# Attention with a mixture of experts: the three groups ahead of the first expert tile overlap one another

## The chip, the cores and the metric

The kernel runs on one core of a Trainium2 chip. The metric is the device time of one execution in microseconds, as the median of several runs. A profile gives the busy intervals of the engines: TensorE (PE, with its weight loads apart as PEld), VectorE (DVE), ScalarE (ACT), GpSimd (POOL) and SyncE (SP, which here only issues DMAs).

## The reference, cut to what matters

```python
x = x + xattn(layernorm(x), ctx, ctx, ...)   # 32 sequences x 128 tokens x 256, 4 heads of 64
x = x + ffn(layernorm(x), router_w, w1, w2)  # 8 experts, 2 for each token, hidden size 1024

# xattn: gates from q and ctx; cs = cumsum(log_sigmoid(fg))
log_D = where(ltr, cs - cs.T, -inf) + ig.T
D = exp(log_D - max(log_D))
C = (q @ k.T / 8) * D
normalizer = maximum(abs(sum(C)), exp(-max_log_D))
h = C / (normalizer + EPS) @ v               # then normed per head, times a scale
# ffn: softmax router, top 2 of 8, h = gelu(x @ w1[e]), y = h @ w2[e], weighed sum
```

## The kernel before, in words

The 32 sequences are worked on in eight groups of four. A group's attention is a long chain over all engines. In the order of a group's own data the pieces are, with their function names (the same name on several engines means the parts of one piece):

- `x_stats`, `x_moments` (DVE), `x_rstd` (POOL), `x_shift` (DVE), `x_norm` (ACT): the layer norm of x, in place in `xin`.
- `turn` (PE, transposes), `turned` (ACT): q transposed. `gates` (PE, 32 small matmuls), `gates_biased` (DVE), `centre` (POOL, the values less their mean), `log_sigmoid` (ACT), `log_forget` (DVE).
- `cumsum`, `decay_turn` (PE), `decay_in`, `cummax`, `rows_right`, `max_token` (DVE; the last three are `middle` there), `rows_left` (ACT), `max_turn` (PE): the terms of the decay.
- `logd` (PE), `decay` (ACT, exp), `scores` (PE, then DVE): C for the four sequences.
- `values` (PE, then ACT: a copy and a square), `head_var` (DVE, six steps), `head_rstd` (POOL), `head_norm`, `head_gamma`, `residual` (DVE): x1.
- `x1_stats`, `x1_moments`, `x1_rstd`, `x1_shift`, `x1_norm`: its layer norm. `router_turn` (PE), `router_turned` (ACT), `logits` (PE), `router` (DVE, 14 steps), `router_exp` (POOL), `meta` (DVE), `ranks`, `counts` (PE), `slots_of`, `list_step` (DVE): which rows go to which expert. `scatter` (POOL, two indirect DMAs for each sequence): the normed rows go to memory, sorted by expert.

Each engine runs its instructions in the order in which they are written; semaphores hold an instruction until its inputs are there, and all that stands behind it on that engine waits too. The order is written out by hand, in `window(w)` for groups 0, 1 and 2 (`STEADY` is 3) and in `step(t, ...)` from t = 3 on. In a step eight expert tiles of 128 rows are computed (`hidden`, `output`, `gelu`, `low`, `weigh`, `add`; 71 tiles in all), and pieces of groups t to t+2 are put between them. In the windows there are no tiles. There the weights of the eight experts are split: each of 16 halves is scaled to 16 bits by ACT (`weights_high`) and its remainder is taken by DVE (`weights_low`); `weights_high(n)` waits for `weights_low(n-1)`. The first `hidden` waits for all 16.

Before, `window(w)` takes group w from its decays to its router, one piece after another: PE has logd(w), scores(w), values(w), turn(w+2), cumsum, decay_turn and max_turn of w+1, gates(w+2), router_turn(w), logits(w). On POOL the eight scatters of group w-1 stand ahead of x_rstd(w+2) and head_rstd(w). On SP, `load_x(g)` waits for turn(g-1), and everything behind it in the queue waits with it.

Of the kernel before, what the change touches and what calls it, by code (L numbers as in the profile page):

```python
# [13 lines left out]
P = 128  # L14
# [67 lines left out]
def build(nc, x, ctx_n, ctx_t, gate_w_in, gate_b_in, gamma, rw_t, w1, w2, cf, cb, pad_rows, out):  # L82
    with ExitStack() as stack:
# [39 lines left out]
        rT = ct[1][:, :, :].rearrange("p a n -> p (a n)").rearrange("p (b j n) -> p b j n", b=G, j=CK)  # L123
# [74 lines left out]
        yo = [sb(f"yo{i}", [P, D]) for i in range(YO)]  # L198
        yx = sb("yx", [P, D])
# [12 lines left out]


# [148 lines left out]
        def _(sp):  # L362
# [68 lines left out]
            for half in range(9, 13):  # L431
                load_w(half)
            sp.dma_start(rows[SPARE:SPARE + P, :], pad_rows).then_inc(s_spare, 16)
            sp.dma_start(out[NT:NT + P, :], pad_rows[:, 0:D]).then_inc(s_spare, 16)
            store_x1(0)
            for half in range(13, 2 * NE):
                load_w(half)
            load_x(3)
            load_x_again(1)
            load_c(2)  # L440
            load_k(3)
            store_x1(1)
            load_c(3)
            load_x(4)
# [33 lines left out]
        def _(pe):  # L478
# [69 lines left out]
            def logd(g, few):  # L548
                if few[0] == 0:
# [4 lines left out]
                    if g < STEADY:  # L554
# [62 lines left out]
            def logits(g):  # L617
# [5 lines left out]
                for b in range(G):  # L623
                    pe.wait_ge(s_rTc, 2 * g + b // 2 + 1)
                    for j in range(CK):
                        mm = pe.matmul(LG[:, b * NE:(b + 1) * NE], rT[:, b, j, :], rwT[:, j, :],  # L626
# [81 lines left out]
            def middle(g):  # L708
                cumsum(g)
                decay_turn(g)  # L710
                max_turn(g)

            def window(w):
                logd(w, (0, 1, 2))
                if w > 0:
                    ranks(w - 1)
                if w > 1:
                    counts(w - 1)
                scores(w, 0)
                logd(w, (3,))  # L720
                scores(w, 1)
                if w == 0:
                    turn(1, 0)
                    turn(1, 1)
                for b in range(G):
                    values(w, b)
                if w == 0:
                    gates(1)
                turn(w + 2, 0)
                turn(w + 2, 1)  # L730
                middle(w + 1)
# [8 lines left out]
            middle(0)  # L740
            pe.wait_ge(s_cbf, 16)
            window(0)
# [4 lines left out]
            def step(t, w, m, f, r):  # L747
                if w is not None:
                    logd(w, (0, 1, 2))
                if r is not None:  # L750
                    ranks(r)
                    if r > 0:
                        counts(r)
                for j in slots(t):
# [5 lines left out]
                    if j == 0 and w is not None:  # L760
# [4 lines left out]
                    if j == 0 and w is not None:  # L765
# [37 lines left out]
        def _(act):  # L803
# [43 lines left out]
            def decay(g, b):  # L847
# [4 lines left out]
                if b == 2:  # L852
# [36 lines left out]
            def router_turned(g, h):  # L889
                act.wait_ge(s_rt, 2 * g + h + 1)  # L890
                if h == 0:
                    act.wait_ge(s_pv, 4 * g + 4)
                act.activation(rT[:, 2 * h:2 * h + 2, :, :],
# [17 lines left out]
            def weigh(i):  # L911
# [3 lines left out]
                act.activation(yx[:, :], YX, ACT.Copy, scale=cw[i % RW][:, :]).then_inc(s_yx, 1)  # L915

            def window(w):
                first = 2 + 5 * w
                floor(w)
                for b in range(G - 1):  # L920
                    decay(w, b)
                weights_high(first)
                if w == 0:
                    x_norm(1, 0)
                    x_norm(1, 1)
                decay(w, G - 1)
                if w == 0:
                    turned(1, 0)
                    turned(1, 1)
                weights_high(first + 1)  # L930
                values(w, 0)
                weights_high(first + 2)
                for b in range(1, G):
                    values(w, b)
                x_norm(w + 2, 0)
                x_norm(w + 2, 1)
                log_sigmoid(w + 1)
                turned(w + 2, 0)
                turned(w + 2, 1)
                rows_left(w + 1)  # L940
                x1_norm(w, 0)
                x1_norm(w, 1)
                weights_high(first + 3)
                router_turned(w, 0)
                router_turned(w, 1)
                if w < 2:
# [723 lines left out]
```

## Time and profile before

| | |
|---|---|
| median of 3 runs | 699.69 us (697.93 to 702.44) |
| the profiled execution | 696.18 us |
| its span, first to last instruction | 694.3 us |
| busy: PE, PEld, DVE, ACT, POOL | 607.4, 480.4, 371.6, 343.2, 265.4 us |
| mean granted TensorE clock | 0.90 |

The span is what the profile's rows are measured in; the execution lasts 1.9 us longer, and the median of the runs 3.5 us longer than this one execution. Times within the rows are counted from the start of the span. A row of a timeline gives the start, the length from the first start to the last end, the engine, the line, the operation, the tiles written and read, how many instructions are merged in it and, in brackets, how long the engine sat idle before it and what released it. The clock column is the granted TensorE clock, 1.00 for 2.4 GHz and 0.50 for 1.2 GHz.

### The profile page before, as it was taken

The numbers are of one execution on the slowest core, as the hardware profiler recorded it, in microseconds if no ns is written. First come the engines' busy times: TensorE is split into PE (matmuls) and PEld (weight loads), VectorE is DVE, ScalarE is ACT, GpSimd is POOL, SyncE is SP. The second block draws the span as 40 slices with busy tenths as digits, with TensorE's granted clock in tenths as the row PEclk, the third lists the DMA queues.
The fourth block names the chain that finished last, engine by engine and source line by source line (L and its number), as shares of the span: only waits on it lengthen the run. The fifth ranks groups of instructions, "written<-read, shape, count | busy, mean of one in ns | idle before, by whom it ended". The sixth has DMA issues, their size and how long they took to land.

```text
span 694.3 us, 18994 instructions
## 1 busy us (share of the span) xinstructions
PE 607.4 (87%) x5885; PEld 480.4 (69%) x5885; DVE 371.6 (54%) x1132; ACT 343.2 (49%) x684; POOL 265.4 (38%) x198
## 2 busy tenths in 40 slices
PE   3775857928899999999899999999899999999993
PEld 3365556626777776777687778678678788787872
DVE  1554664864395539544944584476464444444441
ACT  3453554433457455745564546556345455555551
POOL 0113271542355256434733363444362222222222
PEclk9985555555899999999999999999999999999998
DMA  9995523203324343424333233314244333233222
GB/s 301 380 353 184 199 84 122 70 23 114 109 65 93 60 116 90 102 33 124 106 58 72 46 94 55 85 41 101 42 92 107 59 49 54 47 50 49 48 25 24
DMA packets 44233, 68.14 MB, mean 98 GB/s; under 512 B 4832, under 2 KB 35808, under 8 KB 44000
## 3 DMA queue, kind: packets, MB, share of 16 engines
q1 hardware_dynamic: 30848, 49.09, 22.6%
q0 software_dynamic: 13296, 17.83, 15.1%
q8 instruction: 60, 0.98, 0.6%
q14 instruction: 29, 0.24, 0.1%
HBM read 44.89 MB, written 23.35 MB: 98 GB/s over the span
## 4 chain that ended last, share of the span: by engine, by line
PE 65%; issue 12%; POOL 9%; DVE 6%; ACT 5%; DMA 2%; SPq 0%; DVEq 0%; POOLq 0%; ACTq 0%
PE bank L704 15%; PE bank L690 9%; PE bank L692 8%; PE bank L691 7%; PE bank L705 7%; PE bank L626 3%; POOL rows L1532 3%; PE bank L567 3%; PE bank L652 3%; PE bank L513 2%; PE bank L595 2%; PE bank L580 2%; POOL out L1542 2%; POOL hrs L1519 1%; PE bank L563 1%
## 5 line engine op out<-in xcount | busy, mean ns | idle before, releaser
L690 PE MATMUL bank<-xT,wall 128*128 128x128 f16 x1136 | 209.1, 220 | 9.8 <-issue 9.5
L692 PE MATMUL bank<-xT,wall 128*128 128x128 f16 x1136 | 209.1, 220 | 0.0
L691 PE MATMUL bank<-xT,wall 128*128 128x128 f16 x1136 | 209.1, 220 | 0.0
L704 PE MATMUL bank<-wall,ffn 128*128 x568 | 192.9, 380 | 3.9 <-DVE yo L1309 3.7
L1542 POOL DMA_INDIRECT out<-yo,dst x71 | 114.8, 1618 | 199.7 <-DVE yo L1309 128.4
L900 ACT ACTIVATE ffn<-bank 128x512 f32<-128x512 f32 x142 | 84.7, 596 | 182.3 <-PE bank L692 181.1
L1303 DVE TENSOR_TENSOR gl<-ffn 128x512 f16<-128x512 f32 x94 | 64.9, 690 | 133.5 <-ACT ffn L902 69.9
L690 PEld LDWEIGHTS bank<-xT,wall 128*128 x1136 | 112.5, 99 | 30.3 <-issue 16.7
L692 PEld LDWEIGHTS bank<-xT,wall 128*128 x1136 | 111.3, 98 | 1.9
L691 PEld LDWEIGHTS bank<-xT,wall 128*128 x1136 | 111.3, 98 | 1.1
L705 PE MATMUL bank<-wall,gl 128*128 x376 | 102.4, 272 | 0.0
L704 PEld LDWEIGHTS bank<-wall,ffn 128*128 128x128 f16 x568 | 56.0, 99 | 61.3 <-issue 9.6
L1532 POOL DMA_INDIRECT rows<-rowb,slot x64 | 76.3, 1192 | 55.1 <-DVE rowb L1214 38.9
L902 ACT ACTIVATE ffn<-bank 128x512 f16<-128x512 f32 x142 | 84.0, 591 | 0.0
L1303 DVE TENSOR_TENSOR ffn<-ffn 128x512 f16<-128x512 f32 x48 | 33.1, 690 | 65.6 <-ACT ffn L902 34.7
L705 PE MATMUL bank<-wall,ffn 128*128 x192 | 52.6, 274 | 0.0
L915 ACT ACTIVATE yx<-bank,cw 128x256 f32<-128x256 f32 x71 | 33.7, 474 | 24.5 <-PE bank L705 24.5
L499 PE MATMUL bank<-cst,xin 128*128 128x128 f32 x64 | 12.9, 369 | 37.4 <-ACT xin L811 37.4
L595 PE MATMUL bank<-vt,ct 128*128 128x65 f32 x256 | 39.2, 317 | 2.7 <-DVE ct L1073 2.7
L595 PEld LDWEIGHTS bank<-vt,ct 128*128 128x128 f32 x256 | 37.6, 233 | 4.3 <-DVE ct L1073 3.4
L705 PEld LDWEIGHTS bank<-wall,gl 128*128 128x128 f16 x376 | 36.7, 98 | 3.3
L1309 DVE SCALAR_TENSOR_TENSOR yo<-bank,cw,yx 128x256 f32<-128x256 f32 x71 | 34.2, 482 | 8.5 <-ACT yx L915 4.7
(139 smaller groups left out, 883.9 us busy)
## 6 DMA issues: line engine op xcount, KB each, us to landing
wall<-in_w SPq DMA_DIRECT2D x15, 1024.0 KB, 11.5
xrow<-rows SPq DMA_DIRECT2D x71, 130.0 KB, 2.4
xin<-in_x SPq DMA_DIRECT2D x8, 512.0 KB, 4.4
kT<-in_ctx_t SPq DMA_DIRECT2D x8, 512.0 KB, 4.4
ctn<-in_ctx SPq DMA_DIRECT2D x8, 512.0 KB, 4.2
xres<-in_x SPq DMA_DIRECT2D x8, 512.0 KB, 4.7
out<-xres SPq DMA_DIRECT2D x8, 512.0 KB, 3.6
rows<-in_const_pad SPq DMA_DIRECT2D x9, 130.0 KB, 2.5
```

The costliest lines, as they stand in the source:

```text
L595: mm = pe.matmul(VB[b][:, h4 * (DH + 1):(h4 + 1) * (DH + 1)], ct[b // 2][:, h4 % 2, c0:c0 + P], vt[:, b, h4, :], start=True, stop=True)
L690: pe.matmul(o, hi, xT[i % XT][:, c, :], start=(c == 0), stop=False)
L691: pe.matmul(o, hi, xT[i % XT][:, CK + c, :], start=False, stop=False)
L692: mm = pe.matmul(o, lo, xT[i % XT][:, c, :], start=False, stop=(c == CK - 1))
L704: pe.matmul(YB[:, :], gh[q][:, m4, :], weights(i, w, 2 * D), start=(a == 0 and m4 == 0), stop=False)
L705: mm = pe.matmul(Y, gl[q][:, m4, :], weights(i, w, D), start=False, stop=(a == 1 and m4 == 3))
L900: act.activation(gf[a], HB[a][:, :], ACT.Gelu, scale=1.0 / WSCALE).then_inc(s_gf, 1)
L902: act.activation(gh[(2 * i + a) % HR][:, :, :], HB[a][:, :].rearrange("p (m n) -> p m n", m=4), ACT.Gelu, scale=1.0 / WSCALE).then_inc(s_g ...
L1303: dve.tensor_tensor(gl[q][:, :, :], gf[a].rearrange("p (m n) -> p m n", m=4), gh[q][:, :, :], ALU.subtract).then_inc(s_glo, 1)
L1309: dve.scalar_tensor_tensor(yo[i % YO][:, :], Y, cw[i % RW][:, :], yx[:, :], ALU.mult, ALU.add).then_inc(s_yo, 1)
L1532: pool.indirect_dma_start(out=rows[:, :], out_offset=bass.IndirectOffsetOnAxis(ap=slot[:, k, b:b + 1], axis=0), in_=rowb[:, b, :], in_offs ...
L1542: pool.indirect_dma_start(out=out[:, :], out_offset=bass.IndirectOffsetOnAxis(ap=dst[i % RW][:, 0:1], axis=0), in_=yo[i % YO][:, :], in_of ...
```

## The change

The windows are shifted by half a group. Ahead of window 0 the decays and scores of group 0 are made (a new helper `attend` on PE) and x of group 1 is normed and turned. `window(w)` then holds: values(w) and all that follows to logits(w); in between, the last terms of the decay of group w+1, its logd, decays and scores; gates(w+2); and x_norm(w+3). So at the first tile the scores of group 3 are there, and step 3 holds neither its decays nor its scores; `ranks(2)` and `counts(2)` move behind the first `hidden`. `gates(w+2)` now stands behind `attend(w+1)` and ahead of `router_turn(w)`.

On DVE scores(w+1, 0) stands between head_gamma(w) and residual(w), scores(w+1, 1) ahead of x1_shift(w), and the 15 list steps of window 2 now stand behind head_var. On POOL only four of the eight scatters stand ahead of head_rstd(w), the other four behind it. `weights_low`: three halves are split ahead of window 0, four in each window; in window 2 half 14 comes ahead of `router` and half 15 behind it, and their `weights_high` behind `router_turned(2)`. On SP load_x(3) and load_x(4), the weights 12 to 15 and the contexts are reordered. The transposed rows of the router (`rT`) use the buffers of the expert output in groups 0 to 2, so they no longer share a buffer with the decays.

```diff
 PE
-                logd(w, (0, 1, 2))
+                values(w, 0)
+                values(w, 1)
                 if w > 0:
                     ranks(w - 1)
...
+                    turn(w + 2, 0)
+                    turn(w + 2, 1)
+                    cumsum(w + 1)
+                values(w, 2)
+                if w > 0:
+                    decay_turn(w + 1)
+                values(w, 3)
...
+                max_turn(w + 1)
+                attend(w + 1)
                 gates(w + 2)
                 router_turn(w, 0)
                 router_turn(w, 1)
 DVE, window(w)
+                    decay_in(w + 1)
+                    weights_low(first - 1)
+                    middle(w + 1)
...
+                for n in range(6):
+                    head_var(w, n)
...
                 head_norm(w)
                 head_gamma(w)
+                scores(w + 1, 0, 0)
+                scores(w + 1, 0, 1)
                 residual(w)
                 x1_stats(w)
                 x1_moments(w)
+                scores(w + 1, 1, 0)
+                scores(w + 1, 1, 1)
+                x1_shift(w)
...
+                weights_low(first + 2)
                 for n in range(14):
                     router(w, n)
                 meta(w, 0)
+                if w == STEADY - 1:
+                    weights_low(first + 3)
 POOL, window(w)
-                    for b in range(G):
-                        scatter(w - 1, b)
-                x_rstd(w + 2)
+                    scatter(w - 1, 0)
+                    scatter(w - 1, 1)
                 head_rstd(w)
+                    scatter(w - 1, 2)
+                    scatter(w - 1, 3)
                 x1_rstd(w)
```

## Rows read from the trace of the kernel before

**Rows 1.** Page, the span in 40 slices: granted TensorE clock.
```profile
PEclk9985555555899999999999999999999999999998
```
**Rows 2.** Windows by stage: length, busy us (instructions) by engine, clock, DMA, GB/s.
```profile
26.00:75.60 49.60, 35.04 (x184) 28.76 (x185) 26.12 (x53) 24.61 (x41) 10.53 (x8) 0.72 0.86 301
75.60:121.20 45.60, 32.76 (x151) 26.31 (x152) 27.85 (x66) 21.46 (x35) 20.17 (x15) 0.50 0.30 102
121.20:170.20 49.00, 32.72 (x151) 26.29 (x152) 31.11 (x84) 19.82 (x34) 20.34 (x15) 0.50 0.24 73
...
175.00:187.90 12.90, 11.23 (x118) 9.45 (x119) 4.72 (x15) 6.64 (x16) 3.97 (x4) 0.98 0.46 143
187.90:694.30 506.40, 481.18 (x5225) 378.67 (x5224) 270.10 (x870) 260.71 (x546) 205.81 (x145) 0.99 0.33 68
```
**Rows 3.** Chain that ended last, window 1: start, us, what.
```profile
75.81 0.20 DVE lg L1139
...
83.17 1.21 POOL rows L1532
...
94.37 2.77 POOL rows L1532
...
98.54 2.88 POOL hrs L1519
```
**Rows 4.** Timeline of PE, logits(0) to values(1), at 1.2 GHz.
```profile
72.21 3.56 PE L626 MATMUL bank<-rwT,ct 128*128 128x8 f32 x16 [1.26 <-ACT ct L893]
75.62 1.44 PE L563 MATMUL bank<-cbf 128*128 128x512 bf16 x3
...
80.24 2.08 PE L580 MATMUL bank<-qT,kT 64*128 64x128 f32 x16 [0.94 <-ACT ct L854]
...
84.79 2.08 PE L580 MATMUL bank<-qT,kT 64*128 64x128 f32 x16
86.80 7.09 PE L595 MATMUL bank<-vt,ct 128*128 128x65 f32 x32
```
**Rows 5.** Timeline of PE, gates(3) in window 1: first and last of eight rows.
```profile
105.78 0.99 PE L513 MATMUL bank<-gate_w,qT 128*128 128x12 f32 x4
...
111.74 1.01 PE L513 MATMUL bank<-gate_w,kT 128*128 128x12 f32 x4
```
**Rows 6.** Timeline of PE, gates(1) in window 0: first and last of eight rows.
```profile
43.24 0.57 PE L513 MATMUL bank<-gate_w,qT 128*128 128x12 f32 x4
...
46.34 0.59 PE L513 MATMUL bank<-gate_w,kT 128*128 128x12 f32 x4
```
**Rows 7.** Timeline of DVE, window 0: a weight half, first and last of head_var.
```profile
48.79 2.29 DVE L1080 SCALAR_TENSOR_TENSOR wall<-wall 128x2048 f16<-128x2048 f32 x1 [2.04 <-ACT wall L874]
51.00 0.18 DVE L1220 SCALAR_TENSOR_TENSOR n<-u 128x16 f32<-128x16 f32 x1
...
52.91 0.17 DVE L1240 SCALAR_TENSOR_TENSOR hv<-ss,n 128x16 f32<-128x16 f32 x1
```
**Rows 8.** Timeline of DVE, windows 1 and 2: head_norm, first and last list step.
```profile
103.36 1.22 DVE L1054 TENSOR_TENSOR u<-u,hrs 128x1024 f32<-128x1024 f32 x1
...
141.79 0.42 DVE L1258 TENSOR_TENSOR qT<-ncnt,cst 128x256 f32<-128x256 f32 x1
...
145.54 0.17 DVE L1295 TENSOR_TENSOR dn<-up,te 128x8 f32<-128x8 f32 x1
```
**Rows 9.** Timeline of POOL, window 0: x_rstd(2).
```profile
44.66 2.17 POOL L1495 TENSOR_SCALAR ve<-mv 128x4 f32<-128x4 f32 x1 [12.52 <-DVE mv L1027]
46.92 1.04 POOL L1499 TENSOR_TENSOR rs<-ve,mhalf 128x4 f32<-128x4 f32 x1
```
**Rows 10.** Timeline of ACT: weights_high of one half.
```profile
69.70 1.89 ACT L876 ACTIVATE wall<-wall 128x2048 f16<-128x2048 f32 x1
```
**Rows 11.** Timeline of PE, step 3: first scores and last values of group 3.
```profile
177.23 1.16 PE L580 MATMUL bank<-qT,kT 64*128 64x128 f32 x16
...
184.93 3.14 PE L595 MATMUL bank<-vt,ct 128*128 128x65 f32 x24 [1.55 <-DVE ct L1073]
```

More of the change, by code:

```diff
@@ L430, in _ @@
             load_k(2)
-            for half in range(9, 13):
+            for half in range(9, 12):
+                load_w(half)
+            load_x(3)
+            for half in range(12, 14):
                 load_w(half)
@@ L739, in _ @@
             gates(0)
-            middle(0)
+            cumsum(0)
+            decay_turn(0)
+            max_turn(0)
             pe.wait_ge(s_cbf, 16)
+            attend(0)
+            turn(1, 0)
+            turn(1, 1)
             window(0)
@@ L759, in step @@
                         tile_turn(i + 1)
-                    if j == 0 and w is not None:
+                    if j == 0 and ahead:
+                        ranks(r)
+                        counts(r)
+                    if j == 0 and w is not None and not ahead:
                         scores(w, 0)
@@ L914, in weigh @@
                 after(act, s_yo, i)
-                act.activation(yx[:, :], YX, ACT.Copy, scale=cw[i % RW][:, :]).then_inc(s_yx, 1)
+                act.activation(yx, YX, ACT.Copy, scale=cw[i % RW][:, :]).then_inc(s_yx, 1)
             def window(w):
[L918 to L921, printed above, removed]
+                first = 4 + 4 * w
+                if w == 0:
+                    weights_high(3)
+                values(w, 0)
@@ L926, in window @@
[L926 to L940, printed above, removed]
+                    turned(2, 0)
@@ L941, in window @@
+                    turned(2, 1)
+                    rows_left(1)
+                floor(w + 1)
+                for b in range(G - 1):
+                    decay(w + 1, b)
+                if w < STEADY - 1:
+                    weights_high(first + 1)
+                decay(w + 1, G - 1)
+                if w == STEADY - 1:
+                    turned(w + 2, 0)
+                    turned(w + 2, 1)
                 x1_norm(w, 0)
                 x1_norm(w, 1)
-                weights_high(first + 3)
+                if w == STEADY - 1:
+                    weights_high(first + 1)
@@ L956, in _ @@
             weights_high(1)
+            floor(0)
+            for b in range(G - 1):
+                decay(0, b)
+            weights_high(2)
+            x_norm(1, 0)
+            x_norm(1, 1)
+            decay(0, G - 1)
+            turned(1, 0)
+            turned(1, 1)
             window(0)
@@ L970, in step @@
                     log_sigmoid(m)
-                if w is not None:
+                if w is not None and not ahead:
                     decay(w, G - 1)
@@ L1401, in _ @@
             weights_low(1)
+            x_stats(1)
+            x_moments(1)
+            scores(0, 0, 0)
+            scores(0, 0, 1)
+            x_shift(1)
+            weights_low(2)
+            scores(0, 1, 0)
+            scores(0, 1, 1)
             window(0)
```

166 lines of the change are left out of this document (90 added, 76 removed).

## Prediction

> **What bounds the kernel now.** I read three views. The page's slices and the windows by stage [rows 1, 2] come first: from 187.9 us on PE is busy 481.2 of 506.4 us at a clock of 0.99, so the tiles are bound by PE and little is to be had there. Ahead of that lie three windows of 49.6, 45.6 and 49.0 us in which no engine is full: in window 1 PE has 32.8 of 45.6 us, DVE 27.9, ACT 21.5, POOL 20.2, and half of the PE time is due to the lower clock. That is the picture of a chain, not of a full engine. The chain that ended last [rows 3] says which: logits(0), the router's steps, the eight scatters of the group before (83.17 to 97.14 us), then head_rstd(1), which waited behind them on POOL. The timelines [rows 4 to 9] give the prices.
>
> So the windows are a stretch of about 144 us plus the start of step 3, and the change works only there. I lay the new order out stage by stage, in this execution's time, with PE at 1.2 GHz as it was there.
>
> **Up to 47 us nothing moves.** Ahead of window 0 the new order of every engine is the old one: attend(0), turn(1), x_norm(1) and the halves 0 to 2 stand where they stood.
>
> **Window 0.** x_rstd(2) ends at 47.96 [rows 9]. Before, DVE then still did half 4 (2.29 us) and began head_var at 51.00 [rows 7]. Now half 4 is behind, so head_var (2.1 us, 51.00 to 53.08) runs from 48.1 to 50.2: 2.9 us earlier. Then half 4 (2.3 us) stands ahead of middle(1), and centre(1) runs on POOL next to it. I put max_token(1) at 59.2, where it was at 62.3 (which is 9.3 us behind x_shift; now 11, for half 4). attend(1) starts at 59.4. From logd to the first scores of PE are 4.6 us and to the end of its second scores 11.25 us (75.62 to 86.87) [rows 4]; the first DVE scores start at +6.7, so at 66.1. Here is the price of the new place: head_gamma has ended at 61.5, and DVE stands still until 66.1, with residual(0), x1_stats and the whole router behind it. Scores, residual, stats, moments and the second scores take DVE to 72.0; x1_norm is ready at 74.2. But PE then has gates(2), 70.7 to 77.6: eight rows, 105.78 to 112.75, are 6.9 us [rows 5]. They stood under x1_stats and x1_rstd before and cost nothing; now 3.4 us of them (77.6 less 74.2) lie on the path. router_turn, router_turned and logits (3.56 us [rows 4]) end at 83.2, where logits(0) ended at 75.6. With attend(1) already made, values(1) can start at 83.3 instead of 86.8: gain so far 3.5 us.
>
> **Window 1**, from E = 83.3. ranks(0) must wait for the router's 14 steps on DVE (about 0.22 us each [rows 3]; 4.4 us with the half in front). turn(3), cumsum, values 2 and 3 and max_turn follow, and attend(2) starts at E+11.9 = 95.2. head_var ends at 97.1. Four scatters are now gone from ahead of head_rstd (half of 14 us), which would have it start at once, but weights_low(8) starts on DVE at the same moment. On this core the two exclude each other: the `ve` step of x_rstd(2), one addition on 128x4 elements, took 2.17 us beside a weight half, longer than the power of the same size right behind it, 1.04 us [rows 9]. So head_rstd (2.88 us [rows 3]) ends at 99.4 + 2.8 = 102.2. head_norm (1.22 [rows 8]), head_gamma, scores(2), residual, stats and second scores: 110.1 us. Meanwhile scatters 5 to 8 (5.1 us, about 7 with the same exclusion) hold x1_rstd until 111.3. x1_norm ends at 113.6; gates(3) ends at 115.0 on PE; logits(1) ends at 120.7. Before it ended at 121.2, but with attend(2) still to do (11.2 us). Gain 11.8 us.
>
> The Trainium skill (GPSIMD Engine Reference, section Key points) says that GpSimd shares its SBUF interfaces with VectorE and contends with instructions of two SBUF inputs; the trace agrees, with the 2.17 us above. Without the exclusion this window would be 2.2 us shorter.
>
> **Window 2**, from E = 120.8. The same pattern, with the list steps between head_var and head_norm (141.79 to 145.71, 3.9 us [rows 8]). They lie beside head_rstd, so 1 to 2 us of them remain. logits(2) ends at E+36.2 = 157.0. Then comes a tail that did not exist: weights_high(14) and (15) stand behind router_turned(2), each needs the low half before it, and half 15 stands behind the router's steps on DVE. high(14) 1.9 us [rows 10], low(14) 2.3, router 3.3, low(15) 2.3: the last half ends at E+43.1, 6.9 us behind logits. With 0.7 us for the first tile's table reads as before, the first hidden starts at 164.5. It started at 175.0: 4.8 us behind logits. Gain 10.5 us.
>
> **Step 3.** From the first hidden to that of tile 1 there were 12.9 us [rows 2]: hidden twice, logd(3) and scores (two of 1.16 us [rows 11]), waits for decay and scores, and values in two parts, the last 24 matmuls of 3.14 us behind a wait of 1.55 us. The two scores go (2.3 us), the wait (1.55), and logd and the wait for its exp (2.5, my estimate): 6.5 us stay. To these come ranks and counts (0.5) and about 3 us for the clock: PE will have idled 7 us before this point, so the first hiddens probably run at 1.2 GHz. About 10 us. Gain 2.8 us. Behind that nothing is removed: the same 70 tiles at PE's pace.
>
> **SP and the buffers.** load_x(3) now stands ahead of weights 12 to 15 and waits for turn(2), near 52 us; weights 14 and 15 wait for x1_norm(0), near 74, and are needed near 148. k(4) is there at 112 and needed at 144. load_rows(0) waits for centre(3), near 149, and its tile is turned after 157. No load is on the path. The waits for the shared router buffer are met long before. I cost these at nothing; if one cover fails it is a load of some 4 us, once.
>
> **Sum.** 10.5 + 2.8 = 13.3 us of 696.2, so 682.9 us for such an execution. The median of the runs stands 3.5 us above it, so 686 us, 1.9% faster. About 1% (7 us) is what a measurement of this kernel can tell from no change.
>
> **Rivals.**
> 1. *The windows run at 2.4 GHz.* Gates at the upper level take 3.7 us (43.24 to 46.93 [rows 6]) against 6.9. At that level the gates no longer hold router_turn, logits and turns halve: some 7 us for each of windows 1 and 2 and up to 6 in window 0. Full effect: 666 us; in one window only: 679 us. For it: PE's pauses of 7 and more us before turn(w+2) are gone. Against it: from 72.2 to 93.9 us PE was busy with pauses of about 1 us [rows 4] and the clock stayed at 0.50 [rows 2]. Chance 0.2 for all of its forms.
> The Trainium skill (TensorE: Matmul & The Clock Gate, section Why this matters for your kernels) has it that TensorE reaches its upper clock by steady work and loses it by idle gaps; by that rule this rival would be the rule and not the exception, and the stretch just named speaks against it.
> 2. *The gain is eaten in place.* The waits I priced come out longer: DVE behind scores(w+1, 0), POOL's four scatters in front of x1_rstd, the weight tail. Each is 3 to 7 us per window in my layout, so 3 us more in each of windows 1 and 2 leaves 7 us: 692 us and above. Chance 0.2.
> 3. *Slower: the two chains are serial after all.* If in-order waiting makes windows 1 and 2 as long as before (45.6 and 49.0 us), logits(2) ends at 83.2 + 94.6 = 177.8, the first hidden starts at 185.4 and tile 1 near 195.4 instead of 187.9: 7.5 us slower, 707 us. It decides from the point where the two windows together save under 7.5 of 94.6 us; I have 21. Against it: half of the scatters leave the head's path. Chance 0.07.
> 4. *The change does not reach the end,* since step 3 waits for something else (group 5's x, the scatters of group 2): 696 to 700 us. PE is busy 481 of 506 us from there, so a late piece would have to stop it for 10 us. Chance 0.05; it counts as within 1%.
>
> **How the numbers follow.** My layout has 0.48, and its own range is 681 to 692. The clock rival has 0.2, rival 2 0.2 (half of it above 693), the others 0.12. Leaving out half of each outer case gives 671 to 694. Faster by over 1% (under 692.7): 0.48 + 0.2 + a part of rival 2 = 0.78. Within 1%: 0.15. Slower: 0.07.
>
> **What would show it.** The first hidden near 164 us, tile 1 near 174.5, and 506 us from there to the end. logits(0) near 83, logits(1) near 121, logits(2) near 157. DVE idle for 4 to 5 us between head_gamma(0) and scores(1); gates directly in front of router_turn, with no idle between; weights_low(15) as the last thing before the first hidden, 6 to 7 us behind logits(2). Wrong would be: a granted clock of 1.00 inside windows 1 or 2, a window of 45 us or more, a tile section that grew, or a first hidden released by a load.

## The result, and the profile after

The changed kernel takes 679.5 us (median of 4 runs, 678.85 to 679.74), the kernel before 699.66 us (4 runs beside it, 697.93 to 702.44). The ratio is 0.972, with a 95% interval of 0.968 to 0.976: 2.8% faster, where 1.9% was forecast. The profiled execution took 678.85 us, with a span of 677.1 us and a mean granted clock of 0.905; before it was 696.18, 694.3 and 0.900.

The page of the changed kernel, the granted clock in 40 slices (answers to [rows 1]):

```profile
PEclk9985555555999999999999999999899999999998
```

The windows by stage, cut where the last matmul of logits(0), (1) and (2), the first hidden and tile 1's hidden stand (columns as in [rows 2]):

```profile
26.30:81.80 55.50, 45.06 (x229) 33.77 (x229) 32.69 (x66) 27.88 (x49) 13.82 (x10) 0.68 0.85 296
81.80:117.90 36.10, 32.20 (x151) 26.30 (x151) 27.46 (x66) 19.18 (x33) 21.27 (x15) 0.50 0.32 104
117.90:155.10 37.20, 32.38 (x151) 26.36 (x152) 30.09 (x76) 18.76 (x30) 16.46 (x13) 0.50 0.30 96
155.10:162.10 7.00, 0.51 (x2) 0.10 (x1) 6.12 (x22) 4.00 (x6) 1.01 (x1) 0.50 0.00 0
162.10:170.80 8.70, 8.66 (x91) 8.61 (x92) 2.65 (x15) 3.48 (x9) 2.86 (x3) 0.76 0.44 125
170.80:677.10 506.30, 479.61 (x5225) 377.42 (x5222) 270.77 (x870) 260.69 (x546) 206.76 (x147) 0.99 0.33 69
```

Against [rows 2]: logits(0) ends 6.2 us later than before (attend(1) and gates(2) now stand ahead of it), windows 1 and 2 are 36.1 and 37.2 us long instead of 45.6 and 49.0, and the tile section is 506.3 us, as it was. PE's busy time in the windows has not changed (32.2 and 32.4 us against 32.8 and 32.7), only its idle time has: 12.8 and 16.3 us before, 3.9 and 4.8 us now. Behind logits(2) the tail to the first hidden is 7.0 us where it was 4.8, and tile 1's hidden stands 8.5 us behind the first hidden where it was 12.9. Added up: 9.5 and 11.8 us gained in windows 1 and 2, 4.4 in step 3, 6.2 and 2.2 lost in window 0 and in the tail, together 17.3 us of the 17.2 by which the span is shorter.

The predicted places beside the measured ones, in us:

| place | predicted | measured |
|---|---|---|
| max_token(1) | 59.2 | 58.0 |
| scores(1) on DVE; its idle before | 66.1; 4 to 5 | 65.1; 4.56 |
| logits(0) ends | 83.2 | 81.8 |
| head_rstd(1) ends | 102.2 | 99.7 |
| logits(1) ends | 120.7 | 117.9 |
| logits(2) ends | 157.0 | 155.1 |
| first hidden | 164.5 | 162.1 |
| tile 1's hidden | 174.5 | 170.7 |
| from there to the end | 506 | 506.3 |

Timeline of PE in window 0: the last of the eight rows of gates(2), which answer to [rows 5], then the router and the values that follow.

```profile
75.56 1.01 PE L521 MATMUL bank<-gate_w,kT 128*128 128x12 f32 x4
76.41 1.95 PE L621 MATMUL bank<-cst,rowb 128*128 128x128 f32 x8
78.29 3.55 PE L634 MATMUL bank<-rwT,ybuf 128*128 128x8 f32 x16
81.69 3.66 PE L603 MATMUL bank<-vt,ct 128*128 128x65 f32 x16
```

router_turn (L621) follows the gates with no idle; its input, x1_norm, had been ready since 73.16. So 3.25 us of the gates lie on the path, 3.4 were forecast. Timeline of POOL and then DVE in window 1, what answers to [rows 3] and [rows 9]:

```profile
94.81 4.91 POOL L1578 TENSOR_TENSOR hrs<-hv,mhalf 128x16 f32<-128x16 f32 x1 [0.54 <-DVE hv L1284]
99.92 1.98 POOL L1591 DMA_INDIRECT rows<-rowb,slot  x1 [0.19 <-issue]
...
108.06 1.89 POOL L1571 TENSOR_TENSOR vt<-ctn,gsb 128x1024 f32<-128x1024 f32 x1
94.55 0.18 DVE L1284 SCALAR_TENSOR_TENSOR hv<-ss,n 128x16 f32<-128x16 f32 x1
94.64 2.28 DVE L1124 SCALAR_TENSOR_TENSOR wall<-wall 128x2048 f16<-128x2048 f32 x1
...
108.11 1.87 DVE L1093 SCALAR_TENSOR_TENSOR nm<-mv,rs 128x4 f32<-128x4 f32 x1 [0.64 <-POOL rs L1565]
```

head_rstd (L1578) takes 4.91 us beside the weight half (2.28 us, L1124) where it took 2.88 [rows 3]: 2.0 us more, for the exclusion that the prediction priced at 2.2 us. The last row is one that it did not price: x1_shift (L1093), 128x4 elements, takes 1.87 us beside centre (1.89 us, L1571), which starts 0.05 us ahead of it; in window 0, with nothing on POOL beside it, it takes 0.15. The rule of the Trainium skill that the prediction cited (GPSIMD Engine Reference, section Key points: GpSimd shares its SBUF interfaces with VectorE and contends with its instructions of two SBUF inputs) fits both rows.

Timeline of PE and of DVE at the end of window 2:

```profile
151.53 3.55 PE L634 MATMUL bank<-rwT,ybuf 128*128 128x8 f32 x16 [2.22 <-DVE gsb L1137]
162.13 0.28 PE L698 MATMUL bank<-xT,wall 128*128 128x128 f16 x1 [6.53 <-DVE xT L1358]
148.87 2.29 DVE L1128 SCALAR_TENSOR_TENSOR wall<-wall 128x2048 f16<-128x2048 f32 x1 [2.04 <-ACT wall L896]
151.08 0.20 DVE L1137 TENSOR_TENSOR gsb<-bank,gate_b 128x48 f32<-128x48 f32 x1
...
158.65 2.28 DVE L1128 SCALAR_TENSOR_TENSOR wall<-ffn,wall 128x2048 f16<-128x2048 f32 x1
160.85 0.41 DVE L1358 TENSOR_TENSOR xT<-bank,xT 128x256 f16<-128x256 f32 x1
```

logits(2) waits 2.22 us for gates_biased(4) (L1137), which stands behind weight half 13 on DVE (L1128, 148.87). That half had itself waited 2.04 us for its high part on ACT (L896), and the high part had waited for half 12 on DVE, so it is a chain that goes to and fro between the two engines and starts behind x1_shift(2). The first hidden (L698) waits 6.53 us, behind the router, half 15 (158.65) and tile_low (L1358).

### The profile page after: what moved, and what is told of

Read it like the earlier page. It is cut to its first block, busy times and chain, and to the rows that moved or that the text cites. A ratio compares the mean times of both kernels' runs of the same rounds, so it can differ in the third digit from the quotient of the medians.

```text
span 677.1 us, 18991 instructions
## 1 busy us (share of the span) xinstructions
PE 608.8 (90%) x5885; PEld 482.0 (71%) x5885; DVE 377.4 (56%) x1132; ACT 342.5 (51%) x684; POOL 265.7 (39%) x198
## 4 chain that ended last, share of the span: by engine, by line
PE 65%; issue 14%; POOL 8%; DVE 6%; ACT 4%; DMA 1%; SPq 0%; DVEq 0%; POOLq 0%; ACTq 0%
PE bank L712 15%; PE bank L698 9%; PE bank L700 8%; PE bank L699 8%; PE bank L713 8%; PE bank L521 5%; PE bank L603 3%; PE bank L660 3%; POOL rows L1591 2%; POOL out L1601 2%; PE bank L575 2%; POOL hrs L1578 2%; PE bank L588 2%; PE bank L634 1%; PE bank L507 1%
## 5 line engine op out<-in xcount | busy, mean ns | idle before, releaser
L698 PE MATMUL bank<-xT,wall 128*128 128x128 f16 x1136 | 209.4, 220 | 16.3 <-issue 9.7
L1601 POOL DMA_INDIRECT out<-ybuf,dst x71 | 114.7, 1615 | 201.5 <-DVE ybuf L1353 129.7
L698 PEld LDWEIGHTS bank<-xT,wall 128*128 x1136 | 112.6, 99 | 36.5 <-issue 23.1
L1591 POOL DMA_INDIRECT rows<-rowb,slot x64 | 72.7, 1136 | 55.4 <-DVE rowb L1258 39.4
L937 ACT ACTIVATE ybuf<-bank,cw 128x256 f32<-128x256 f32 x71 | 33.6, 474 | 24.5 <-PE bank L713 24.5
L603 PEld LDWEIGHTS bank<-vt,ct 128*128 128x128 f32 x256 | 37.4, 229 | 2.5 <-DVE ct L1117 1.7
L713 PEld LDWEIGHTS bank<-wall,gl 128*128 128x128 f16 x376 | 36.7, 98 | 3.4
L1353 DVE SCALAR_TENSOR_TENSOR ybuf<-bank,cw,ybuf 128x256 f32<-128x256 f32 x71 | 34.3, 483 | 8.5 <-ACT ybuf L937 8.2
L1578 POOL TENSOR_TENSOR hrs<-hv,mhalf 128x16 f32<-128x16 f32 x8 | 25.5, 3190 | 32.7 <-DVE hv L1284 32.7
```

Of the source, the lines that this page charges most:

```text
L603: mm = pe.matmul(VB[b][:, h4 * (DH + 1):(h4 + 1) * (DH + 1)], ct[b // 2][:, h4 % 2, c0:c0 + P], vt[:, b, h4, :], start=True, stop=True)
L698: pe.matmul(o, hi, xT[i % XT][:, c, :], start=(c == 0), stop=False)
L713: mm = pe.matmul(Y, gl[q][:, m4, :], weights(i, w, D), start=False, stop=(a == 1 and m4 == 3))
L1578: pool.tensor_tensor(hrs[:, :], hv[:, :], mhalf[:, :], ALU.pow).then_inc(s_hrs, 1)
L1591: pool.indirect_dma_start(out=rows[:, :], out_offset=bass.IndirectOffsetOnAxis(ap=slot[:, k, b:b + 1], axis=0), in_=rowb[:, b, :], in_offs ...
L1601: pool.indirect_dma_start(out=out[:, :], out_offset=bass.IndirectOffsetOnAxis(ap=dst[i % RW][:, 0:1], axis=0), in_=yo[i % YO], in_offset=N ...
```

## The experiments

The changed kernel is the base of each, but for the second, which starts from the kernel before. The medians of the kernel before beside them were 697.3 to 697.9 us. The changed kernel itself was not run again beside them, so a difference to it of 2 or 3 us is believed only where the places in the trace show it too. Ratios are to the kernel before, with 95% intervals; the last three columns are starts in the profiled execution. Up to logits(0) the executions differ by 1 to 2 us of themselves, in stretches that an edit doesn't touch, so what an edit of windows 1 and 2 does is read from logits(0) on.

| kernel | median us | ratio | span | logits(0) | first hidden | tile 1 |
|---|---|---|---|---|---|---|
| kernel before | 699.7 | | 694.3 | 72.2 | 175.0 | 187.9 |
| changed kernel | 679.5 | 0.972 (0.968 to 0.976) | 677.1 | 78.3 | 162.1 | 170.7 |
| scatters first | 687.7 | 0.987 (0.986 to 0.989) | 684.8 | 79.4 | 170.6 | 178.8 |
| before, scatters split | 697.3 | 0.999 (0.997 to 1.001) | 696.1 | 73.2 | 175.6 | 189.6 |
| half of the gates | 676.4 | 0.971 (0.969 to 0.972) | 674.7 | 75.7 | 158.1 | 167.4 |
| centre late | 677.2 | 0.973 (0.971 to 0.976) | 675.3 | 77.6 | 160.1 | 169.0 |
| half early | 676.1 | 0.969 (0.966 to 0.971) | 673.3 | 78.1 | 159.1 | 167.1 |
| both, and tile_low early | 671.7 | 0.962 (0.960 to 0.964) | 670.1 | 78.4 | 155.4 | 163.9 |
| group 3 late | 684.3 | 0.978 (0.974 to 0.983) | 688.8 | 80.4 | 163.1 | 179.8 |
| the same, again | 686.2 | 0.984 (0.980 to 0.987) | 682.5 | 80.6 | 163.3 | 177.6 |
| fill | 673.0 | 0.964 (0.962 to 0.967) | 670.4 | 71.6 | 156.3 | 164.4 |
| all and fill | 665.9 | 0.955 (0.952 to 0.959) | 664.2 | 71.6 | 149.1 | 157.8 |
| fill in the gates too | 671.1 | 0.962 (0.959 to 0.966) | 668.8 | 73.4 | 153.9 | 162.3 |
| residual first | 679.1 | 0.974 (0.970 to 0.977) | 678.1 | 79.7 | 163.5 | 171.7 |

**All scatters ahead of head_rstd again.**

```diff
                     x_rstd(2)
                 else:
-                    scatter(w - 1, 0)
-                    scatter(w - 1, 1)
+                    for b in range(G):
+                        scatter(w - 1, b)
                 head_rstd(w)
                 if w == 0:
                     centre(1)
-                else:
-                    scatter(w - 1, 2)
-                    scatter(w - 1, 3)
```

> The changed kernel with one part undone: in windows 1 and 2 all eight scatters stand ahead of head_rstd on POOL again. Theory A, the split of the scatters is a large part of the gain: in the changed kernel the first scatter starts at 88.3 us, eight take 14 us (that is what they took before), so head_rstd(1) would start near 102.5 instead of 94.8 and end 5.7 us later; of that x1_rstd, which no longer waits behind four scatters, gives nothing back as long as gates end behind it. Window 1 about 5 us longer, window 2 5 to 6 us longer: 689 to 691 us. Rival B, POOL's order is off the path, as its idle time of 60 per cent would have it: 679 to 681 us.

Measured: 687.7 us, 8.2 more than the changed kernel (7.7 by the spans). Timeline of POOL and DVE, the last scatter, head_rstd(1), head_norm(1):

```profile
100.47 0.96 POOL L1591 DMA_INDIRECT rows<-rowb,slot  x1 [0.30 <-issue]
101.45 2.93 POOL L1578 TENSOR_TENSOR hrs<-hv,mhalf 128x16 f32<-128x16 f32 x1
104.42 1.23 DVE L1098 TENSOR_TENSOR u<-u,hrs 128x1024 f32<-128x1024 f32 x1 [6.36 <-POOL hrs L1578]
```

head_rstd starts at 101.45 instead of 94.81 (1.1 us of this stands ahead of window 1 already), with no wait of its own: it stands behind the scatters, and DVE idles 6.36 us for it where it idled 2.83. From logits(0) to logits(2) are 80.6 us instead of 73.2: 3.6 us more in window 1, 3.8 in window 2. In the new order the split is worth 7 to 8 of the 20 us.

**The split alone, in the kernel before.**

```diff
                     x_rstd(1)
                 else:
-                    for b in range(G):
-                        scatter(w - 1, b)
+                    scatter(w - 1, 0)
+                    scatter(w - 1, 1)
                 x_rstd(w + 2)
                 head_rstd(w)
+                if w > 0:
+                    scatter(w - 1, 2)
+                    scatter(w - 1, 3)
```

> The kernel before with one part of the change alone: in windows 1 and 2 four of the eight scatters stand behind head_rstd. Theory A, as the prediction read the chain of the kernel before (eight scatters, then head_rstd): head_rstd starts up to 5 us earlier in each window and the kernel gains 5 to 9 us: 691 to 695 us. Rival B, before the change head_rstd was bound by its own input as well: head_var ended at 98.3 us, 0.2 us ahead of head_rstd's start in window 1, and at 147.7 against 147.8 in window 2, so the scatters had only just ceased to bind. Then the split gains nothing, and four scatters behind head_rstd delay x1_rstd by up to 1 us in each window: 699 to 702 us.

Measured: 697.25 us over 10 runs against 697.34 for the kernel before. The same split that is worth 7 to 8 us above is worth nothing here. Timeline of POOL in this kernel, head_rstd(1) and (2):

```profile
99.30 2.90 POOL L1519 TENSOR_TENSOR hrs<-hv,mhalf 128x16 f32<-128x16 f32 x1 [5.18 <-DVE hv L1240]
148.34 2.90 POOL L1519 TENSOR_TENSOR hrs<-hv,mhalf 128x16 f32<-128x16 f32 x1 [9.02 <-DVE hv L1240]
```

and of DVE and POOL in the kernel before, which the prediction did not set side by side:

```profile
98.12 0.18 DVE L1240 SCALAR_TENSOR_TENSOR hv<-ss,n 128x16 f32<-128x16 f32 x1
98.52 2.90 POOL L1519 TENSOR_TENSOR hrs<-hv,mhalf 128x16 f32<-128x16 f32 x1
...
147.52 0.17 DVE L1240 SCALAR_TENSOR_TENSOR hv<-ss,n 128x16 f32<-128x16 f32 x1
147.78 2.90 POOL L1519 TENSOR_TENSOR hrs<-hv,mhalf 128x16 f32<-128x16 f32 x1 [3.68 <-DVE hv L1240]
```

Before, head_var(1) ended at 98.30 and head_rstd(1) started at 98.52, so the queue in front of it (the scatters, then x_rstd(3)) was late by 0.2 us at most; in window 2 POOL even waited 3.68 us for head_var. Freed of four scatters, POOL waits 5.18 and 9.02 us. In the changed kernel head_var(1) ends at 94.73; in the run with all scatters first it ends at 95.86, and the scatters hold POOL until 101.43. The overlap brings head_var forward against the router's end, and only then is a queue of scatters in the way.

**Half of the matmuls of gates(2) to gates(4) left out.**

```diff
-                    for j in range(2 * CK):
+                    for j in range(2 * CK) if not 2 <= g < STEADY + 2 else (0, 2 * CK - 1):
```

> The changed kernel with half of the matmuls of gates(2), (3) and (4) left out (two of four for each sequence, so the gates of groups 2 to 4 lack half of their inputs): each gates piece takes about 3.5 us instead of 6.9. Theory A, gates in front of router_turn cost what the prediction says: in window 0 x1_norm ends at 73.2 and gates at 76.4, so router_turn and the end of window 0 move up by 3.2 us; in windows 1 and 2 x1_norm and the weight halves bind nearly as late, so there 0 to 1 us each. Sum 3.2 to 5 us: 674.5 to 676.5 us. Rival B, another wait (the weight half in front of the router on DVE) binds right behind in window 0 too: under 1.5 us, 678 us and above.

The gates of groups 2 to 4 lack half of their inputs in this kernel. Measured: 676.4 us, 3.2 less (2.4 by the spans). Timeline of PE, windows 0 and 2:

```profile
73.54 1.95 PE L621 MATMUL bank<-cst,rowb 128*128 128x128 f32 x8
75.65 3.55 PE L634 MATMUL bank<-rwT,ybuf 128*128 128x8 f32 x16 [0.16 <-DVE gsb L1137]
...
141.80 2.10 PE L621 MATMUL bank<-cst,rowb 128*128 128x128 f32 x8 [1.69 <-ACT rowb L905]
147.51 3.56 PE L634 MATMUL bank<-rwT,ybuf 128*128 128x8 f32 x16 [3.62 <-DVE gsb L1137]
```

In window 0 router_turn comes 2.9 us earlier, about the 3.25 us that the gates held it. In windows 1 and 2 what the gates give up turns into waits: for x1_norm (L621, 1.97 and 1.69 us) and for gates_biased (L634, 0.94 and 3.62 us, where it was none and 2.22). From the second scores on PE to logits are 10.6 and 13.0 us, in the changed kernel 10.7 and 13.0. So PE's gates bind window 0 alone; in window 2 it is the weight halves on DVE and ACT.

**centre behind x1_shift,** so that the small instruction doesn't run beside the large one.

```diff
                 if w > 0:
+                    pool.wait_ge(s_nm2, w + 1)
                     centre(w + 1)
```

> The changed kernel with one wait added: centre(w+1) on POOL waits for x1_shift(w) in windows 1 and 2. In the changed kernel's trace x1_shift, a step of 128x4 elements, takes 1.87 us in windows 1 and 2 beside centre and 0.15 us in window 0. Theory A, the two engines exclude each other: x1_shift takes 0.15 us, x1_norm starts 1.7 us earlier in both windows; in window 1 gates end at 112.4 and x1_norm at 112.1, so nothing is gained there; in window 2 the chain of the last weight halves starts behind x1_shift, so the first tile starts 1.7 us earlier: 677.8 us. Rival B, x1_shift is slow for another reason (its inputs come late): it stays at 1.9 us and the time at 679.5 us.

Measured: 677.2 us, 2.3 less, of which the trace shows 1.6 as the edit's: from logits(1) to logits(2) are 35.6 us instead of 37.2, and window 1 is as long as before (36.0). The other 0.7 stands ahead of logits(0), where nothing was changed. Timeline of DVE and of POOL, window 1:

```profile
107.43 0.16 DVE L1093 SCALAR_TENSOR_TENSOR nm<-mv,rs 128x4 f32<-128x4 f32 x1 [0.64 <-POOL rs L1565]
107.67 3.88 POOL L1571 TENSOR_TENSOR vt<-ctn,gsb 128x1024 f32<-128x1024 f32 x1 [0.28 <-DVE nm L1093]
```

x1_shift is back at 0.16 us; centre now takes 3.88 us beside the next weight half, which nobody waits for. A wait was added, and window 2 became shorter by what x1_shift had lost there.

**A weight half moved from the tail into DVE's idle stretch of window 0,** so that none stands behind router(2).

```diff
                 head_gamma(w)
+                if w == 0:
+                    weights_low(first + 1)
+                    first += 1
                 scores(w + 1, 0, 0)
...
                 meta(w, 0)
-                if w == STEADY - 1:
-                    weights_low(first + 3)
```

ScalarE's high halves move with it, and each later half comes one place earlier.

> The changed kernel with one weight half more split in window 0: half 5 on DVE between head_gamma(0) and scores(1), where DVE sat idle for 4.56 us, and every later half one place earlier, so that none is left behind the router of window 2. Theory A, the first tile waits for the tail of weight halves: weights_low(15) (2.3 us) goes from behind router(2); the first tile then waits for tile_low behind the router, 2.2 us earlier; window 0 itself does not change, since the half fits into the idle time. 677.3 us. Rival B, the half in window 0 pushes scores(1) and the chain of window 0 back by as much, or DVE and ACT are the bound in window 2 whatever the order: 679 to 681 us.

Measured: 676.1 us, 3.4 less (3.8 by the spans). Timeline of DVE in window 0 and of PE at the first hidden:

```profile
60.28 2.28 DVE L1131 SCALAR_TENSOR_TENSOR wall<-wall 128x2048 f16<-128x2048 f32 x1
64.92 1.29 DVE L1120 SCALAR_TENSOR_TENSOR ct<-bank,ct 128x512 f32<-128x512 f32 x2 [2.35 <-PE bank L588]
...
159.12 0.29 PE L698 MATMUL bank<-xT,wall 128*128 128x128 f16 x1 [3.81 <-DVE xT L1361]
```

The idle of 4.56 us takes the half (2.28 us), and the scores behind it start no later; the wait of the first hidden falls from 6.53 to 3.81 us, which is 2.7 of the 3.8 us.

**Both edits, and tile_low(0) ahead of router(2).**

```diff
+                if w == STEADY - 1:
+                    tile_low(0)
                 for n in range(14):
                     router(w, n)
...
             window(2)
-            tile_low(0)
```

> The changed kernel with three edits that each take away one wait found in its trace: the half in window 0 (as in e4_half_early), centre behind x1_shift (as in e3_centre_late), and tile_low(0) ahead of router(2) on DVE, so that the first tile no longer waits for the 14 router steps and meta. If the waits are in series, as the trace shows them (router and last half 5.4 us between logits and the first tile, x1_shift 1.7 us), the first tile starts 5 to 6.5 us earlier than at 162.1 us: 673 to 674.5 us. If they cover each other: 676 us and above.

Measured: 671.7 us, 7.8 less (7.0 by the spans), with 1.27 us left of the wait before the first hidden. Window 2 is 1.6 us shorter, as with centre late, and the stretch from logits(2) to the first hidden is 5.3 us shorter, of which the early half gave 2.7 in its own run; by difference the early tile_low gives 2.5, though it has no run of its own. The gains add up.

**Group 3's logd, decays and scores back in step 3,** where they were before.

```diff
                 max_turn(w + 1)
-                attend(w + 1)
+                if w < STEADY - 1:
+                    attend(w + 1)
```

The same condition stands on ScalarE and VectorE, and the three of them do the work in step 3 instead.

> The changed kernel with group 3 taken out of the overlap: its logd, decays and scores are in step 3 again, as before the change. Theory A: step 3 gets its 12.9 us from the first hidden to that of tile 1 back, where the changed kernel has 8.7 us: 4.2 us lost; window 2 loses scores(3) on DVE (2.5 us), so x1_norm and the chain of weight halves behind it come 1.5 to 2.5 us earlier. Net 2 us slower than the changed kernel: 681.5 us. Rival B: attend(3) is free in window 2 (PE has it in time that it would idle), so the whole 4.2 us are lost: 683.7 us. Rival C: PE has the work to do at some time anyway, and at the higher clock in step 3 it is cheaper: 679 us or less.

> The same kernel as e6_group3_late once more, since its four times lay between 681.3 and 690.6 us. There the second half of values(3) and the first hidden of tile 1 ran at half pace behind a wait of 1.55 us in step 3 (5.39 us for 24 matmuls). If that wait lets the clock fall in some executions only, the times spread again over 5 to 9 us, the lowest near 681.3 us; a median of 682 to 685 us. If the first look was disturbed: all within 2 us of 681.5 us.

Measured: 684.3 us, but spread from 681.3 to 690.6, and in the second run of it 686.2 (682.3 to 687.7). By the medians this part is worth 4.8 to 6.7 us. In both profiles 2.1 to 2.3 us of the difference stand ahead of logits(0), where the edit changes nothing: there values(0) and gates(1) run at half the pace (gates(1) at 1.01 us a row instead of 0.59). From logits(0) on, window 2 is 1.1 us shorter without the work of group 3, and step 3 is 14.3 and 16.7 us long instead of 8.5, so the part is worth 4.6 us in one execution and 7.1 in the other, more than theory A or B gave it. Timeline of PE in the second profile, step 3:

```profile
174.87 2.89 PE L603 MATMUL bank<-vt,ct 128*128 128x65 f32 x24 [1.55 <-DVE ct L1119]
177.60 0.22 PE L698 MATMUL bank<-xT,wall 128*128 128x128 f16 x1
```

The wait of [rows 11] is back (1.55 us), and the values at the pace of 2.4 GHz. In the first profile the same 24 matmuls took 5.39 us behind the same wait, and tile 1 came at 179.8: there PE fell to half its pace in that stretch. That is one explanation of the spread; two profiles don't prove it.

**Fill: matmuls that nobody needs where PE idled** (128x512 bf16, into a bank that nobody reads at that time), to see what the lower clock costs.

```diff
+            def fill(n):
+                for _ in range(n):
+                    pe.matmul(XB[:, :].rearrange("p (h n) -> p h n", h=NH), cbf[:, B_IDENT:B_IDENT + P], mask,
+                              start=True, stop=True)
```

16 of them stand ahead of turn(2), 12 ahead of max_turn(1), 4 or 2 ahead of attend, 3 ahead of the scores (ahead of the second ones only for groups 2 and 3), and 3 ahead of ranks.

> The changed kernel with extra matmuls (128x512 bf16, results overwritten) in PE's idle places of the three windows: 16 and 12 in window 0 where PE sits idle 3.5 and 3 us, 2 to 4 in the waits for decays, scores and ranks. It tests the prediction's first rival. In the changed kernel PE is busy 32.2 of 36.1 us in window 1 and the granted clock is 0.50 all through. If more work in PE's idle places lifts the clock to 1.00 in the windows, gates take 3.7 us instead of 6.9 and the windows get 5 us and more shorter each: 665 to 675 us. If the clock stays at 0.50, each extra matmul costs 0.4 us where it isn't covered: 680 to 686 us.

Measured: 673.0 us, 6.5 less. Windows of this kernel (columns as in [rows 2]) and timeline of PE, the last two rows of gates(2), logits(0) and the second scores of group 2:

```profile
52.00:64.00 12.00, 10.45 (x67) 4.91 (x67) 9.40 (x11) 6.20 (x10) 4.70 (x2) 1.00 0.82 286
64.00:84.00 20.00, 18.58 (x115) 16.74 (x111) 15.59 (x51) 12.31 (x23) 5.52 (x6) 0.66 0.60 200
84.00:92.00 8.00, 6.45 (x37) 2.57 (x37) 5.55 (x11) 6.46 (x10) 7.07 (x5) 1.00 0.25 93
92.00:128.00 36.00, 28.60 (x150) 23.70 (x151) 27.92 (x76) 16.11 (x30) 20.86 (x16) 0.62 0.27 89
```

```profile
67.02 0.68 PE L521 MATMUL bank<-gate_w,qT 128*128 128x12 f32 x4
67.55 1.01 PE L521 MATMUL bank<-gate_w,kT 128*128 128x12 f32 x4
...
71.62 3.55 PE L634 MATMUL bank<-rwT,ybuf 128*128 128x8 f32 x16 [0.79 <-DVE gsb L1148]
...
97.58 2.08 PE L588 MATMUL bank<-qT,kT 64*128 64x128 f32 x16 [5.40 <-DVE ct L1128]
```

The clock is at its upper level (2.4 GHz) in 52 to 64 and in 84 to 92 us, stretches that hold the added matmuls, and the first six rows of gates(2) run at a pitch of 0.45 us. Then it falls to the lower one (1.2 GHz) towards the end of the gates, without an idle PE: the row at 67.55 takes 1.01 us where the first six took 0.59 to 0.61.

All that the fill gives, it gives in window 0: logits(0) starts at 71.6 us instead of 78.3, 6.7 us earlier. Windows 1 and 2 are 36.7 and 37.4 us long, no shorter than the 36.0 and 37.2 of the changed kernel. In window 1 the time that PE gains at the upper level between 84 and 92 us it waits for DVE afterwards (5.40 us ahead of the second scores, L588, where the changed kernel waits 1.53), and gates(3) and gates(4) run at 1.01 us a row again.

**All of it: the three edits and the fill.**

> e5_all_three with the extra matmuls of e7_fill. The first took 7.8 us off the changed kernel (shorter tail in front of the first tile), the second 6.5 us (clock up in parts of windows 0 and 1). If the two are independent, as one acts on ACT, DVE and POOL behind x1_shift and the other on PE: 671.7 less 6 = 665 to 666 us. If the tail of weight halves binds so hard that PE's gains in window 2 are lost: 667 to 669 us. Over 670 us would say that they hide each other.

Measured: 665.9 us (665.89 to 667.16), 0.955 of the kernel before and some 2% under the changed kernel: the best version of the study. Timeline of PE, the last row of gates(2) and router_turn(0):

```profile
67.47 0.59 PE L521 MATMUL bank<-gate_w,kT 128*128 128x12 f32 x4
68.74 2.10 PE L621 MATMUL bank<-cst,rowb 128*128 128x128 f32 x8 [0.68 <-ACT rowb L916]
```

Here all eight rows of gates(2) run at the upper level, and the clock is at the lower one right behind them (0.50 from 68.1 to 80 us).

**A filling matmul also behind each sequence's gates and logits,** to hold the clock through them.

```diff
                                        start=(j == 0), stop=(j == 2 * CK - 1))
+                    if 0 < g < STEADY + 2:
+                        fill(1)
```

> e9_all_and_fill with one further extra matmul behind each sequence's gates and logits. In e7_fill's trace the clock goes down in the course of gates, though PE is not idle for a moment there. Theory A, it is the small matmuls (12 and 8 columns) that let it fall: with a 512-column matmul between them the clock stays at 1.00 through gates(2), gates take 3.7 + 4 x 0.22 = 4.6 us instead of up to 6.9, router_turn and logits are short as well, and each window gains 2 to 4 us over e9: 658 to 663 us. Rival B, four more matmuls change nothing for the clock and cost 4 x 0.43 us each time: 2 to 4 us slower than e9.

Measured: 671.1 us, 5.1 more than without. Timeline of PE, gates(2):

```profile
68.28 0.51 PE L528 MATMUL bank<-gate_w,qT 128*128 128x12 f32 x4
68.64 0.70 PE L528 MATMUL bank<-gate_w,kT 128*128 128x12 f32 x4
69.57 0.87 PE L528 MATMUL bank<-gate_w,qT 128*128 128x12 f32 x4
70.28 1.01 PE L528 MATMUL bank<-gate_w,kT 128*128 128x12 f32 x4
```

The clock falls in the gates all the same, in the sixth of their eight rows; without these matmuls the eight rows took 0.59 to 0.61 us each. In gates(1) it falls too, in the second row. So the matmuls cost their own time and hold nothing.

**residual, x1_stats and x1_moments of group 0 ahead of scores(1).**

```diff
+                if w == 0:
+                    residual(w)
+                    x1_stats(w)
+                    x1_moments(w)
                 scores(w + 1, 0, 0)
                 scores(w + 1, 0, 1)
...
```

> The changed kernel with residual(0), x1_stats(0) and x1_moments(0) ahead of scores(1, 0) on DVE in window 0, where DVE sits idle for 4.56 us. Theory A, the idle time costs nothing: x1_shift(0) stands behind scores(1, 1), which waits for PE until 69.6 us, and router_turn(0) waits for gates(2) until 76.4 us in any case; nothing moves: 679 to 680 us. Rival B, as the prediction put it, these 4.6 us are a price on the path: 675 us.

Measured: 679.1 us, no difference. Timeline of DVE, the second scores and x1_shift:

```profile
71.07 1.29 DVE L1117 SCALAR_TENSOR_TENSOR ct<-bank,ct 128x512 f32<-128x512 f32 x2 [3.27 <-PE bank L588]
72.27 0.15 DVE L1093 SCALAR_TENSOR_TENSOR nm<-mv,rs 128x4 f32<-128x4 f32 x1
```

The idle moves behind the stats, and nothing else moves: x1_shift starts 12.5 us behind the first matmul of attend(1) in both kernels (59.78 to 72.27 here, 58.39 to 70.89 in the changed one), because it stands behind the second scores in both orders and PE sets when those come. attend(1) itself starts 1.4 us later in this execution because values(0) and gates(1) ahead of it ran at half the pace (gates(1) at 1.01 us a row instead of 0.59). The 4.56 us of idle cost nothing there. An order with x1_shift ahead of the second scores was not run.

## Why the prediction came out 6.5 us too high

**The layout held.** Two windows shorter by the waits that the overlap removes, a tile section that doesn't change, a tail of weights ahead of the first hidden: each was there, within 4 us at every place of the table. Rival 1 did not occur (clock 0.50 in both windows), nor rivals 2, 3 and 4.

**The sizes.** Of the 6.5 us (686 less 679.5), 3.8 are in the layout: window 0 was 1.4 us shorter than laid out (1.2 of it up to max_token), window 1 1.4 shorter (1.0 up to the end of head_var, 0.4 behind it in spite of the 1.7 that x1_shift lost beside centre), window 2 1.0 longer (36.2 against 37.2: logits(2) waits for gates_biased behind half 13, and x1_shift beside centre), the tail 0.5 shorter, step 3 8.5 us where "about 10" stood. The x1_shift is the whole of what window 2 has too much: with centre late it is 35.6 us. In step 3 it is the term "about 3 us for the clock", for which the prediction had no row: 33 matmuls of the first two hiddens stand 0.105 us apart and the rest 0.055, which makes 1.6 to 1.7 us instead of 3.

**The step that failed outright** is the last: "The median of the runs stands 3.5 us above it." That distance was added to the forecast as if it belonged to the kernel. The larger part of it belonged to the one profiled execution of before and the three timed ones it was held against (696.18, against 697.93 to 702.44): with 7 to 13 executions beside the experiments the median of before is 697.3 to 697.9, 1.2 to 1.8 us above the profiled one, and for the changed kernel it is 0.65 us. This is 2.9 of the 6.5 us, and together with the layout it explains them.

**A reading that was wrong without costing anything** is the one of [rows 3]. "head_rstd(1), which waited behind them on POOL" is true of the order and false as a cause: head_var, which it needs, ended only 0.2 us before head_rstd started. Had the forecast been for the split alone, it would have promised several us where there were none (ratio 0.999). It did no harm since the layout was built from start times and durations and not from that chain.

**"Here is the price of the new place"**, said of DVE's idle of 4 to 5 us, had the right size and place and the wrong name: two runs show that nothing waits for DVE there. It holds a weight half for free, and doing the residual and the stats in it gains nothing.

**Rival 1 and the clock.** From 63.01 to 85.35 us the timeline of the changed kernel shows no idle PE (busy 22.34 of 22.34 us), the granted clock is 0.50, and the gates take 1.01 us a row. The Trainium skill (TensorE: Matmul & The Clock Gate, section Why this matters for your kernels) ties the upper clock to steady work without idle gaps; here the trace does not agree, since the clock neither rises in that stretch nor holds to the end of the gates in the filled kernel, where PE is not idle either. What the filled runs add: the upper level in parts of window 0, up to the gates, is worth 6.7 us with the price of the added matmuls taken off, where the rival had "up to 6 in window 0". Its 7 us for each of windows 1 and 2 stay untested, because no run has the upper level in gates(3) or gates(4), and where a part of window 1 had it, nothing was gained. What holds the clock through the gates and behind them stays open; one large matmul behind each sequence's does not.

**What the pieces are worth**, by the runs: the split of the scatters 7.3 us (by the windows) to 8.2 (by the medians) in the new order and nothing without it, group 3's part 4.6 to 7.1 us. The rest, some 5 to 8 of the 20 us, goes to the overlap of groups 1 and 2 itself by difference alone; no run shows it by itself. The two pieces were each taken away from the whole, so their sum needn't be exact.

## What to carry to other kernels

A chain that goes through a queue says who stood in front, not who was late: before a gain is put on a shorter queue, look when the input of the waiting instruction was ready, because the slack may be 0.2 us. When two chains are overlapped, lay out again which small instruction of one engine falls beside a large one of another, which low-priority block (here a weight half) stands in front of an instruction that another engine waits for, and which idle stretch can take it; these gave 7.8 us more after the change. Before the cost of a lower clock is taken off, ask who waits for the engine: the same upper clock gained 6.7 us in window 0 and nothing in window 1, where PE then waited for DVE. Forecast in the scale of the median, from the ratio of layouts, and don't carry the distance of one profiled execution over as if it were part of the kernel.

## What the runs showed of the hardware that was not expected

- A DVE instruction on 128x4 elements takes 1.87 us when POOL has begun one on 128x1024 elements 0.05 us earlier, and 0.15 us alone; the other way round POOL's centre takes 3.88 us instead of 1.89 beside a weight half of 2.28 us. In these pairs whichever starts second ends last.
- TensorE's clock fell in the course of fp32 matmuls of 12 columns that followed one another without idle (rows of 0.59 us, then 1.01), after stretches at the upper level; in another run it held through eight such rows and was lower right behind them.
- In the two traces with group 3 late and in the one with the residual first, the record of the granted clock reads 1.00 through the windows while the gates run at the slow pace (rows of 1.01 us, 0.85 apart). In these three values(0) and gates(1) are slow too, and attend(1) starts 1.4 to 2.3 us later than in the changed kernel. Where record and pace differ, the durations of the matmuls are to be believed.
